# Adding x to the output projection's bias in an accumulating transfer instead of on GpSimd

## The reference

```
q = rotary((x @ Wq + bq) per head);  k = rotary(x @ Wk + bk);  v = x @ Wv + bv
ctx = softmax(q k^T / sqrt(32)) v
x = layernorm(x + (ctx @ Wo + bo))
x = layernorm(x + bitlinear(sigmoid(bitlinear(x, w1)) * bitlinear(x, w2), w3))
bitlinear(x, w) = x @ clip(round(w / (mean|w| + eps)), -1, 1).T
```

## Time and profile before

| | |
|---|---|
| median of three runs | 636.84 us |
| the profiled execution | 638.78 us |
| its span | 637.0 us |
| mean granted TensorE clock | 0.949 |
| TensorE busy | 557.5 us (88%) |
| VectorE busy | 479.6 us (75%) |
| ScalarE busy | 413.2 us (65%) |
| GpSimd busy | 289.3 us (45%) |
| bytes moved by transfers | 92.11 MB |

### The profile page before, as it was taken

The page is one execution under the profiler, slowest core; times in us unless marked ns, Lnnn a source line. Parts: engine busy times, 40 slices in busy tenths (PEclk is TensorE's granted clock), DMA queues, the critical chain, the costliest instruction groups (busy, mean ns, idle before and its releaser), DMA issues.

```text
span 637.0 us, 9128 instructions
## 1 busy us (share of the span) xinstructions
PE 557.5 (88%) x2964; PEld 276.1 (43%) x2964; DVE 479.6 (75%) x659; ACT 413.2 (65%) x841; POOL 289.3 (45%) x386
## 2 busy tenths in 40 slices
PE   6777968969779899999779999989689999989994
PEld 2443554425344344444434444444344444444441
DVE  1777877647989787987989897897989898446333
ACT  1697796647778686865777887664878889033310
POOL 1308798887457142656556312855546310021001
PEclk9799979988969899998989999989989999999997
DMA  7490624038979997988999995977989989400001
GB/s 289 140 330 7 222 79 141 1 74 167 157 152 229 164 185 115 172 163 175 180 164 237 190 186 111 185 169 144 163 186 186 176 154 193 83 16 34 0 1 66
DMA packets 217102, 92.11 MB, mean 145 GB/s; under 512 B 204384, under 2 KB 205536, under 8 KB 216544
## 3 DMA queue, kind: packets, MB, share of 16 engines
q1 hardware_dynamic: 209952, 77.61, 58.4%
q0 software_dynamic: 6144, 12.60, 9.5%
q10 hardware_dynamic: 960, 1.33, 0.6%
HBM read 20.20 MB, written 4.19 MB: 38 GB/s over the span
## 4 chain that ended last, share of the span: by engine, by line
PE 59%; DVE 16%; issue 8%; DMA 7%; ACT 6%; POOL 2%; SPq 2%; POOLq 0%; DVEq 0%; ACTq 0%
PE a_ps L1221 10%; PE a_ps L1152 6%; PE s_ps L1234 5%; PE s_ps L1261 5%; DVE p_all L968 5%; PE b_ps L1221 5%; PE e_ps L1221 4%; DMA pt_sb<-p_all 4%; PE c_ps L1313 3%; PE b_ps L1206 3%; DVE sh_sb L961 3%; PE b_ps L1234 3%; PE c_ps L1299 3%; DMA late<-in_w 2%; PE e_ps L1152 2%
## 5 line engine op out<-in xcount | busy, mean ns | idle before, releaser
L695 ACT ACTIVATE p_all<-s_ps,sh_sb 128x512 f32<-128x512 f32 x192 | 130.2, 683 | 86.2 <-DVE sh_sb L961 81.7
L961 DVE TENSOR_REDUCE sh_sb<-s_ps 128x2 f32<-128x1024 f32 x96 | 116.9, 1217 | 40.1 <-PE s_ps L1261 40.1
L968 DVE SCALAR_TENSOR_TENSOR p_all<-p_all 128x1024 f16<-128x1024 f32 x96 | 128.6, 1340 | 2.5 <-ACT p_all L703 2.3
L703 ACT ACTIVATE p_all<-p_all 128x1024 f16<-128x1024 f32 x96 | 101.7, 1059 | 2.0
L1221 PE MATMUL a_ps<-late,q 128*128 128x512 f16 x352 | 84.6, 384 | 6.2 <-ACT th L666 4.6
L1261 PE MATMUL s_ps<-k_st,q_st 128*128 128x512 f32 x192 | 84.3, 521 | 5.5 <-ACT p_all L695 2.8
L416 POOL DMA_DIRECT2D q_st<-hi x96 | 49.5, 518 | 66.5 <-PE s_ps L1261 40.7
L531 POOL TENSOR_SCALAR rstd<-mv 128x1 f32<-128x1 f32 x32 | 9.5, 298 | 141.5 <-DVE mv L928 141.5
L1152 PE MATMUL a_ps<-xT_sb,wq_sb 128*128 128x512 f32 x104 | 58.4, 696 | 6.2 <-DMA wq_sb<-in_wq 6.2
L509 POOL TENSOR_TENSOR rot<-raw,table_sb 128x512 f32<-128x512 f32 x20 | 26.9, 1344 | 64.1 <-ACT raw L626 60.6
L1221 PEld LDWEIGHTS a_ps<-late,q 128*128 128x128 fp8e4 x352 | 31.9, 98 | 49.9 <-issue 8.7
(11 more groups left out here) (149 smaller groups left out, 986.8 us busy)
## 6 DMA issues: line engine op xcount, KB each, us to landing
q_st<-hi POOLq DMA_DIRECT2D x96, 64.0 KB, 2.9
q_st<-lo POOLq DMA_DIRECT2D x96, 64.0 KB, 3.5
late<-in_w SPq DMA_DIRECT2D x2, 2816.0 KB, 11.2
xT_sb<-in_xT SPq DMA_DIRECT2D x8, 512.0 KB, 5.3
late<-in_x SPq DMA_DIRECT2D x4, 1024.0 KB, 6.5
out<-late SPq DMA_DIRECT2D x12, 256.0 KB, 3.0
late<-in_w SPq DMA_DIRECT2D x2, 1408.0 KB, 7.0
q_st<-hi SPq DMA_DIRECT2D x32, 64.0 KB, 2.0
```

The lines of the kernel that those rows point to most:

```text
L695: act.activation(p_pair[n][:, t % 2, :], pair_banks(h * PAIRS + t // 2)[:, t % 2, :], ACT.Exp, bias=sh_sb[:, 2 * n + t % 2:2 * n + t % 2 + ...
L703: act.activation(p_half[n][:, 0, :], p_pair[n].rearrange("p t k -> p (t k)"), ACT.Copy, scale=P_SCALE).then_inc(p_hi, 1)
L961: dve.tensor_reduce(sh_sb[:, 2 * n:2 * n + 2], pair_banks(h * PAIRS + i), AX.X, ALU.min).then_inc(maxed, 2)
L968: dve.scalar_tensor_tensor(out=p_half[n][:, 1, :], in0=p_pair[n].rearrange("p t k -> p (t k)"), scalar=P_SCALE, in1=p_half[n][:, 0, :], op ...
```

## The change

SyncE now copies the bias row, four times side by side, from its place in SBUF into `xb` (`load_bias`, at the places of `load_x`). GpSimd then waits for that and issues one transfer of 1 MB that reads x from HBM and adds it to what is in `xb` (`add_rows`, at the place of the first `add_bias`). The four additions go. `attended` waits for the transfer's 16 instead of for one of four counts. For sequence 0, SyncE also waits until the bias has been loaded.

```diff
-            def load_x(s):
-                sp.dma_start(xb, x[s, :, :].rearrange("(t p) d -> p t d", p=P)).then_inc(x_in, 16)
+            def load_bias(s):
+                sp.dma_start(xb, bo_sb.unsqueeze(1).broadcast_to([P, TT, D])).then_inc(x_in, 16)
...
-            load_x(0)
+            sp.wait_ge(b_in, 16)
+            load_bias(0)
...
-                        load_x(b)
+                        load_bias(b)
...
-            def add_bias(s, t):
+            def add_rows(s):
+
                 pool.wait_ge(x_in, (s + 1) * 16)
-                pool.tensor_tensor(xb[:, t, :], xb[:, t, :], bo_sb, ALU.add).then_inc(bo_added, 1)
+                pool.dma_start(xb, x[s, :, :].rearrange("(t p) d -> p t d", p=P),
+                               accum_op=ALU.add).then_inc(bo_added, 16)
...
-            for t in range(TT):
-                add_bias(0, t)
+            add_rows(0)
             cosines(1, "q0")
...
                 cosines(b, "q3")
-                add_bias(b, 0)
+                add_rows(b)
                 stack(pool, b, 10)
-                add_bias(b, 1)
                 stack(pool, b, 11)
-                add_bias(b, 2)
-                add_bias(b, 3)
...
-                dve.wait_ge(bo_added, s * TT + t + 1)
+                dve.wait_ge(bo_added, (s + 1) * 16)
```

## The result

The changed kernel takes 646.96 us, the median of four runs (646.31 to 648.26), against 636.71 (634.85 to 637.56) of the kernel before: a ratio of 1.0168, 95% interval 1.0139 to 1.0196. That is 10.2 us slower, where 12.1 were forecast. On another chip, with the experiments (e11), it was 1.0131 (1.0091 to 1.0172). The profiled execution took 646.43 us, with a span of 644.6, 7.6 more than before.

What follows compares the result with a forecast made beforehand. It took transfers at the late transposes to be the bound in two of three stages, nearly in the third. Terms 10.0 + 1.7 + 0.4 = 12.1 us on 638.78 gave 650.9, or 648.9 on the median; range 638.5 to 665.

Steps and rivals of the forecast that it cites:

- Nothing to gain on GpSimd: All stages: removing GpSimd's four additions per sequence gains nothing, since whatever is saved becomes more waiting for TensorE's scores.
- VectorE's low halves: Stage 3: without contention from GpSimd's additions, 0.7 us can come back, counting only where the transpose wait doesn't open.
- GpSimd's issue: GpSimd, each sequence: issuing the 1 MB transfer costs 0.518 to 8.3 us, hidden; taken as 0, 1.5 per stage kept for range.
- The rival of late stacks: GpSimd's issue takes far over 8.3 us, stacks come late for step 18: 1.5 us a stage, 653.4 us; chance 0.05.
- SyncE's copy at no extra cost: SyncE's bias copy inside SBUF replaces the load of x: taken as 0, at worst 2.4 us slower.
- The transfer's price: DMA engines, stages 1 and 2: the adding megabyte delays the already late transpose by 5.0 us each.
- the dear rival: Adding doubles the transfer's work: 10.1 us each in stages 1 and 2, 5.5 in stage 3, to 664.2 us; chance 0.15.
- Stage 1 and 2: it goes to TensorE undiminished: ScalarE's wait is already open and TensorE can't catch up, so each extra microsecond counts: +5.0 each, +10.0.
- Clock: TensorE, stage 2: idle time over 6 us lowers the granted clock for the matmuls behind it, +1.7 us.
- Stage 3: The transpose there lands in 10.5 us against room of 10.1, so the wait adds 0.4 us.
- Faster: SyncE's copy finishes earlier, transpose waits shrink and VectorE's 0.7 returns: -2.6 us, 634.2 us; chance 0.08.
- Hidden in the gaps: Addition costs 2.6 us, half hidden while engines wait for HBM: +1.9 us, 638.7 us; chance 0.17.

Runs made afterwards that it cites:

- e11: The changed kernel run once more, unaltered, on another chip against the kernel before: ratio 1.0131, 644.76 us.
- e3: The kernel before without GpSimd's sixteen additions (bias left out of the result), x still loaded by SyncE: ratio 0.9965, 634.27 us.
- e5: The changed kernel with the adding transfer of stages 1 to 3 moved behind stack 13, about step 20: ratio 1.0232, 651.27 us.
- e1: The changed kernel with GpSimd's transfer as a plain copy of x over the bias, no addition: ratio 1.003, 637.69 us.
- e2: The changed kernel with GpSimd's transfer as a plain copy of x and SyncE's bias copy gone too: ratio 0.998, 634.80 us.
- e8: The changed kernel with the adding transfer cut to the first two of four row tiles, half the bytes: ratio 1.0005.

## Why the prediction was right, point by point

- **Nothing to gain on GpSimd.** Not right in size. On GpSimd's own path the additions cost nothing, but they and their wait for x held the stack transfers back until these fell among the transposed x and the late transpose. Without them stage 1 is 2.7 us shorter in e3's trace, 1.25 us of it idle time and the rest the clock; the whole kernel is 1.7 to 2.2 us faster. The step that failed is "whatever is saved becomes more waiting", which looked at the engine and not at what it issues. The changed kernel can't have this gain, since its stacks still stand behind a wait for the copy. In e5, whose adding transfer and its wait stand behind stack 13, steps 12 to 20 are 1.9 and 0.9 us shorter than before in stages 1 and 2, which fits, but in stage 1 only 0.5 us of it is idle time (2.51 for 2.98) and the rest the clock.
- **VectorE's low halves, 0.7 us.** They did come back: at the places of the additions all take 1.22 us, where they took up to 1.92 in stage 3. It bought nothing in the changed kernel, as the sum had it, since the wait behind it opened; in e3, where it doesn't, stage 3 is 0.4 us shorter and not 0.7.
- **GpSimd's issue, 0.5 to 8.3 us.** 1.38 to 1.55 us. It hid nothing and cost nothing, as taken; ScalarE's wait for stacks went from 4.3 to 4.7 us. The rival of late stacks falls.
- **SyncE's copy at no extra cost.** Right by landing: 5.3, 5.9 and 6.9 us in stages 1 to 3, where x took 6.1, 5.8 and 7.0. The second megabyte as a whole, with the stacks' wait for it, costs some 3 us (e1 less e2).
- **The transfer's price, 5.0 us at the late transpose.** The term that was over-sized: the landing grew by 2.6 and 3.8 us in stages 1 and 2, to 15.5 and 14.7, where 16 to 18 were to show it. The bare engine time is 6.8 us, between the forecast and the dear rival's 10.1, so the 5.0 was too low for what the transfer takes and too high for what reaches the transpose; that these two errors partly cancel is luck. It had been taken from q0's stack transfers as the price of a plain copy of a megabyte, and a plain copy took 3.4 us alone (e1). Of the 6.8 the landings show mostly what adding puts on top of copying (2.6 and 2.5 us); that the rest is covered while the engines wait for the transposed x is argued. That the cost doesn't go with the bytes (e8) was near one of the rivals ("half of it falls into time in which the engines wait") and not in the forecast.
- **Stage 1 and 2: it goes to TensorE undiminished.** Right: 2.4 and 3.2 us more idle, and the traces stay apart by as much until the end of the stage.
- **Clock, 1.7 us in stage 2.** Right: 2.1, and nothing of the kind new in stages 1 and 3.
- **Stage 3, 0.4 us.** Right: 0.2, with a landing of 11.35 for the estimated 10.5; ScalarE waits 1.15 us and TensorE 0.37. The room was well put, 10.2 us for the middle of 10.1. The late transpose isn't the one that was priced, at 5.5 us, but that of step 14, which took 5.4 before.
- **Sum.** By the traces 2.7 + 5.3 + 0.2 = 8.2 us for the forecast 5.0 + 6.7 + 0.4 = 12.1; by the medians 10.2. The 2 us between these two are within what single executions of this kernel differ by, and I haven't found a place for them; e11 has 8.0 by its trace and 8.3 by its ratio. So the mechanism, the place and the direction are shown, and the sum was some 4 us too high for what the traces can place.
- **Rivals.** Dear: refuted, the late transposes grew by 2.6 and 3.8 us and not 10.1. Faster: refuted, the transpose landed later. Hidden in the gaps: holds for half the bytes (e8), not for all.

## What to carry to other kernels

An accumulating transfer is a load that books the DMA engines for twice the time (6.8 us against 3.4 for a megabyte here), so price it where it will be in flight, against the transfer that is already waited for, and look for a stretch without such a transfer before giving up the idea: four adding megabytes beside transposes made this kernel 10 us slower; made ahead, in HBM, they cost nothing, and the kernel kept the 2 to 4 us that leaving out GpSimd's additions gives. Freeing an engine that isn't on the path can still pay or cost through the transfers it issues; look at when they go out, not only at when the engine next has work. And a transfer has room up to some landing time, 10.2 us for a transpose in stage 3 here; half of the adding transfer cost nothing that could be told, the other half cost it all.

## What the runs showed of the hardware that was not expected

- A megabyte added to SBUF took 6.8 us of the 16 engines and landed in 9.4 us alone; copied, 3.4 and 6.1. Its packets were half as large (528 against 275 for the same bytes).
- Two queues in flight together got nearly the same number of packets through, 283 and 291 in 4 us of the changed kernel. With 256 bytes in a packet of the transpose and 2 KB in one of the adding transfer, that was 0.12 MB against 0.60 MB.
- A 1 MB transfer from GpSimd's queue beside transposes sometimes brought both to a near stop, 0.14 MB in 4 us with the engines booked full (e5); whether plain or adding, the kernels with the transfer at step 20 were 2% slower. It was seen in some stages and not in others with the same order of issues, and what decides on it stays open.
- A GpSimd issue took 1.38 to 1.55 us for the adding megabyte and 0.82 to 0.99 for the plain one (e1), where 64 KB take 0.52.
- The granted clock fell behind an idle TensorE of 2.06 us (e2, 0.59) and of 2.98 us, and stayed at 1.00 behind one of 2.85 (e1), all at the same place of stage 1. How long TensorE stands idle doesn't settle it alone.
- VectorE's low half took 1.92 us beside GpSimd's additions and 1.22 at the same step without them.
